# Second attention layer of a four-layer kernel: first rows fetched in the experts' part, split parts stored by feature and stacked in three transfers a side on two queues

## The reference, cut to what matters

```
x = x + attn_a(layernorm(x), ...)      # landmark attention
x = x + ffn(layernorm(x), ...)         # router and three experts
x = x + attn_b(layernorm(x), Wq, Wk, Wv, Wo)
x = x + ffn(layernorm(x), ...)

def attn_b(x, Wq, Wk, Wv, Wo):         # 16 heads of 16 features
    q, k, v = (x @ W.T).reshape(B, T, 16, 16) for W in (Wq, Wk, Wv)
    q, k = apply_rotary(q), apply_rotary(k)
    scores = einsum('bhqd,bhkd->bhqk', q, k) * 16 ** -0.5    # causal mask
    out = einsum('bhqk,bhkd->bhqd', softmax(scores), v)
    return out.reshape(B, T, 256) @ Wo.T
```

## Time and profile before

| | us |
|---|---|
| median of 3 runs (2417.48 to 2418.22) | 2417.69 |
| profiled execution, its time | 2412.47 |
| profiled execution, its span | 2410.7 |
| end of the first experts' stage, start of `layer_b` | 1427.6 |
| first scores of `layer_b` (PE) | 1470.2 |
| first turned scores of `layer_b` (PE) | 1514.4 |
| end of `layer_b` | 1968.0 |

### The profile page before, as it was taken

The page is one execution under the profiler, slowest core; times in us unless marked ns, Lnnn a source line. Parts: engine busy times, 40 slices in busy tenths (PEclk is TensorE's granted clock), DMA queues, the critical chain, the costliest instruction groups (busy, mean ns, idle before and its releaser), DMA issues. The chain is left out here.

```text
span 2410.7 us, 49639 instructions
## 1 busy us (share of the span) xinstructions
PE 2150.9 (89%) x19430; PEld 1743.2 (72%) x19430; DVE 1486.6 (62%) x3884; ACT 1027.4 (43%) x1986; POOL 680.2 (28%) x772
## 2 busy tenths in 40 slices
PE   7799999999999998798789964889999878987998
PEld 7688888888888887677589952445544447766998
DVE  2565664746566474588646645777777628874665
ACT  4343434434343443344245521455555543433554
POOL 3210110201011111266512224433333215662222
PEclk8899999999999999899889987899999989998999
DMA  7300000000000000421657765544455226113775
GB/s 238 119 19 11 10 10 10 19 2 19 10 11 10 10 1 25 110 66 58 241 158 228 236 168 94 90 83 86 84 87 87 43 87 204 42 44 117 231 225 139
DMA packets 155905, 212.84 MB, mean 88 GB/s; under 512 B 51656, under 2 KB 140000, under 8 KB 150368
## 3 DMA queue, kind: packets, MB, share of 16 engines
q1 hardware_dynamic: 142140, 191.51, 27.9%
q0 software_dynamic: 12864, 17.38, 4.4%
q10 hardware_dynamic: 672, 0.79, 0.2%
HBM read 141.93 MB, written 67.69 MB: 87 GB/s over the span
## 5 line engine op out<-in xcount | busy, mean ns | idle before, releaser
L2382 DVE CUSTOM_DVE_ANT_0 bank<-bank,b_raw_masks 128x512 f32<-128x512 f32 (+3 forms) x512 | 239.2, 518 | 140.1 <-PE bank L2609 134.7
L2505 ACT ACTIVATE b_probsT<-bank 128x512 f32<-128x512 f32 x320 | 181.0, 603 | 171.3 <-PE bank L2609 140.1
L2114 PE MATMUL bank<-e_hT_hi,k_rwkv 128*128 128x256 f32 x1088 | 213.0, 282 | 2.8 <-DVE e_hT_lo L2017 2.8
L2114 PEld LDWEIGHTS bank<-e_hT_hi,k_rwkv 128*128 128x128 f32 x1088 | 176.1, 190 | 3.6 <-DVE e_hT_lo L2017 3.6
L2609 PE MATMUL bank<-b_k_stacked,b_q_stacked 96*128 96x512 bf16 (+3 forms) x512 | 127.3, 313 | 54.2 <-DMA b_k_stacked<-scratch_b_parts 26.9
L789 POOL TENSOR_TENSOR probs<-probs,rcp 128x512 f32<-128x512 f32 x64 | 66.9, 1045 | 345.3 <-DVE rcp L658 345.3
L2128 PE MATMUL bank<-v_rwkv_hi,e_hidden_hi 128*128 (+1 forms) x544 | 153.7, 282 | 0.0
L2128 PE MATMUL bank<-v_rwkv_hi,e_hidden_lo 128*128 (+1 forms) x544 | 153.6, 282 | 0.0
L2128 PE MATMUL bank<-v_rwkv_lo,e_hidden_hi 128*128 (+1 forms) x544 | 152.0, 279 | 0.0
L2114 PE MATMUL bank<-e_hT_lo,k_rwkv 128*128 128x256 f32 x544 | 151.5, 279 | 0.0
L2075 ACT ACTIVATE e_relu<-bank,k_bias 128x256 f32<-128x256 f32 x272 | 113.5, 470 | 71.6 <-PE bank L2114 58.0
(11 more groups left out here) (360 smaller groups left out, 6102.7 us busy)
## 6 DMA issues: line engine op xcount, KB each, us to landing
k_rwkv<-scratch_k SPq DMA_DIRECT2D x32, 2048.0 KB, 7.4
scratch_b_parts<-b_part SPq DMA_DIRECT2D x96, 128.0 KB, 1.9
b_q_stacked<-scratch_b_parts SPq DMA_DIRECT2D x96, 128.0 KB, 4.3
b_k_stacked<-scratch_b_parts SPq DMA_DIRECT2D x96, 128.0 KB, 4.4
e_rows<-scratch_rows SPq DMA_DIRECT2D x34, 258.0 KB, 7.6
scratch_rows<-f_hq SPq DMA_DIRECT2D x16, 516.0 KB, 8.4
x_tokens<-in_x_dram SPq DMA_DIRECT2D x8, 512.0 KB, 8.4
scratch_x_out<-x_tokens SPq DMA_DIRECT2D x8, 512.0 KB, 2.9
```

Of the source, the lines that this page charges most:

```text
L2114: last = nc.tensor.matmul(data[:, half * ROWS:(half + 1) * ROWS], ff.k_part(i % 2, a)[:, k, at:at + P], hT[b][:, i % 2, k], start=n == 0, ...
L2382: last = nc.vector.tensor_tensor_reduce(data[:, at:at + size], data[:, at:at + size], raw_masks[:, T - size:T], -1.0, LARGEST, ALU.add, AL ...
L2505: nc.scalar.activation(probsT[:, ring, u], fl.data("st", pair, u)[:], ACT.Exp, scale=DB ** -0.5).then_inc(fl.released("st", pair, u), 1)
```

## The change

Seven edits:

1. `experts`, run 0: SP waits for the same additions as GpSimd and issues x of batch 0 there, on a semaphore of the core, `x_first`, that `layer_b` waits for.
2. Loads of `layer_b`: masks first, on a semaphore of their own; then wq, wk, cosines and sines (`loaded`); then wv and wo (`late_loaded`). ScalarE waits for the masks, PE for the identity alone, the q/k and v products of batch 0 and the maxima for what they read.
3. Batch 0's second q and k products move from slots -8, -7 to -10, -9, its v products from -7, -6 to -10, -9 (`FIRST`, `inputs_at`), with everything that follows them.
4. `parts_out` is laid out [feature, head, token] instead of [head, feature, token]: a feature's eight heads are 8 KB in a row.
5. `Q_PARTS` and `K_PARTS_B` are reordered so that one transfer takes three, two and one parts (`RUNS`). On the q side these are neighbouring parts; on the k side one part repeated 3, 2 and 1 times by a broadcast dimension in front.
6. The first half's stores and stacked transfers: q's on SP's queue, k's on ScalarE's queue, after the middle part of the first keys. Later halves stay on SP.
7. Counts of semaphores follow.

The core of the diff:

```diff
+            if run == 0:
+                for p in range(2):
+                    sp.wait_ge(*added(p, of_parity(p)))
+                sp.dma_start(cols(core.x, 0, XB).rearrange("p (t c) -> p t c", c=C),
+                             x_out[0:T, :].rearrange("(t p) c -> p t c", p=P)).then_inc(core.x_first, 16)
...
-Q_PARTS, K_PARTS_B = (0, 0, 1, 1, 0, 2), (0, 1, 0, 1, 2, 0)
+Q_PARTS, K_PARTS_B = (0, 1, 2, 0, 1, 0), (0, 0, 0, 1, 1, 2)
+RUNS = ((0, 3), (3, 2), (5, 1))
...
+FIRST = {"qk": (-12, -11, -10, -9), "v": (-10, -9)}
 FRONT = {"stats": -15, "xn": -14, "xT": -13, "qk": (-12, -11, -8, -7), "v": (-7, -6), "max": (-2, 2)}
...
-        parts_out, max_out = scratch("b_parts", (B * 4, 3, P, T)), ...
+        parts_out, max_out = scratch("b_parts", (B * 4, 3, DB, HEADS_H, T)), ...
...
-        x_back = [sem(f"b_x_back{n}") for n in range(B)]
+        x_back = [core.x_first] + [sem(f"b_x_back{n}") for n in range(1, B)]
...
+        def inputs_at(slot, kind):
+            first = [(0, i) for i, at in enumerate(FIRST[kind]) if at == slot]
+            return first + [(n, i) for n, i in steps_at(slot, FRONT[kind]) if n]
...
+        by_head = lambda at, c: parts_out[at, c].rearrange("d h t -> h d t")
+        def stack(eng, side, b, at):
+            for first, n in RUNS:
+                src = parts_out[at, 0:n] if side == 0 else parts_out[at, K_PARTS_B[first]].unsqueeze(0).to_broadcast([n, DB, HEADS_H, T])
+                eng.dma_start(stacked[side][b][first * DB:(first + n) * DB, :, :],
+                              src.rearrange("c d h t -> (c d) h t") if side == 0 else src).then_inc(stack_loaded[b], 16)
...
                     for c in range(3):
-                        sp.dma_start(parts_out[at, c], parts[c][:, at % 2]).then_inc(s["parts_stored"], 16)
+                        sp.dma_start(by_head(at, c), parts[c][:, at % 2]).then_inc(s["parts_stored"], 16)
...
-                    for row, c in enumerate((Q_PARTS, K_PARTS_B)[side]):
-                        sp.dma_start(stacked[side][b][row * DB:(row + 1) * DB, :, :],
-                                     parts_out[at, c].rearrange("(h d) t -> d h t", d=DB)).then_inc(stack_loaded[b], 16)
-
-                load_x(0)
+                    stack(sp, side, b, at)
+
+                sp.dma_start(raw_masks[:], dram["masks"]).then_inc(s["masks_loaded"], 16)
+                for dst, name in ((wq, "WqT"), (wk, "WkT")):
+                    sp.dma_start(dst[:], dram[name].rearrange("(k p) n -> p k n", p=P)).then_inc(s["loaded"], 16)
+                for dst, name in ((cos, "cos"), (sin, "sin")):
+                    sp.dma_start(dst[:], dram[name]).then_inc(s["loaded"], 16)
+                for dst, name in ((wv, "WvT"), (wo, "WoT")):
+                    sp.dma_start(dst[:], dram[name].rearrange("(k p) n -> p k n", p=P)).then_inc(s["late_loaded"], 16)
                 core.clear_last(sp)
...
                 for c in range(3):
-                    sp.dma_start(parts_out[0, c], parts[c][:, 0]).then_inc(s["first_stored"], 16)
-                sp.wait_ge(s["keys_split"], 1)
...
-                sp.wait_ge(s["first_stored"], 96)
+                    sp.dma_start(by_head(0, c), parts[c][:, 0]).then_inc(s["first_stored"], 16)
+                sp.wait_ge(s["first_stored"], 48)
+                stack(sp, 0, 0, 0)
...
-                    ready(full("s", pair, u))
+                    ready(full("s", pair, u), (s["masks_loaded"], 16))
...
                     nc.scalar.activation(parts[1][:, at % 2], rotated[:, at % 2], ACT.Copy).then_inc(s["mid_done"], 1)
+                    if (n, step) == FIRST_KEYS:
+                        act.wait_ge(s["keys_split"], 1)
+                        for c in range(3):
+                            act.dma_start(by_head(1, c), parts[c][:, 1]).then_inc(s["keys_stored"], 16)
+                        act.wait_ge(s["keys_stored"], 48)
+                        stack(act, 1, 0, 1)
...
                     if kind in ("qk", "v"):
+                        if n == 0:
+                            pe.wait_ge(*((s["loaded"], LOADS) if kind == "qk" else (s["late_loaded"], LATE)))
...
-                pe.wait_ge(s["loaded"], LOADS)
-                pe.wait_ge(s["consts_done"], CONSTS)
+                pe.wait_ge(core.ident_loaded, 16)
...
+                                pe.wait_ge(s["consts_done"], CONSTS)
+                                pe.wait_ge(stack_loaded[half % STACK_BUFS], STACK_DMAS * 16 * (half // STACK_BUFS + 1))
```

## The result

The changed kernel takes **2565.69 us** (median of 4 runs, 2562.2 to 2567.11) against 2417.95 for the kernel before beside it (4 runs, 2417.48 to 2422.31): 1.0607 times as long, 95% interval 1.0591 to 1.0624. Forecast were 2459 us and a range of 2394 to 2500. The sign was right, and so was the main mechanism, few DMA engines for the k stack; the size was wrong by a factor of 3.6: +148 instead of +41 us.

What follows compares the result with a forecast made beforehand. TensorE was taken to set the steady pace of the second attention layer, with stacked transfers a hidden second bound. Stops of 62 less 15 back gave +47, head -6: +41 us, 2459 us on the median, range 2394 to 2500.

Steps and rivals of the forecast that it cites:

- few DMA engines for the k stack: Stacked k transfers, whose source leads with the repeat, run on 3, 2 and 16 engines: 14.4 us against 7.6.
- a second bound, hidden by 1.7 us of cover: Steady part: first scores of each half need all stacked transfers; a k stack later than 1.7 us stops TensorE, fifteen times.
- The first transfer's packets, 0.45 us each: First k transfer of a stack: 16 packets of 8 KB at 0.45 us, between 0.32 and 0.68, together 7.2 us.
- The rival with full collisions: First k transfer at 0.68 us a packet, SP's later stores caught behind engines 0 and 1: 2515 us, chance 0.05.
- The stores, "1 gained": Steady part: k stores sit less long behind the quicker q stack, 1 us a half gained (0 to 1.4).
- Forecast were 62: Steady part: TensorE's stops over fifteen halves, 15 x 13.4 - 138.8 = 62 us.
- Part comes back: 15: Steady part: VectorE catches up during stops, shortening TensorE's waits for it by about 1 us a half, 15 us.
- The head, -6: Layer's head: first scores stay at 1470.0, but from there to pair 4 takes 20 us instead of 25.75: -6 us.
- the step for the moved work: Head: batch 0's second half and v fill the time before first scores; pair 4 follows after 20 instead of 25.75 us.
- The rival with 16 engines: All stacked transfers use 16 engines, the repeat being folded or split on issue: 2399 us, chance 0.17.

Runs made afterwards that it cites:

- head alone: The changed kernel with the old layout and the old six stacked transfers a side, head edits kept: 2409.15 us, 0.9947 of the kernel before.
- k in pairs: The changed kernel with k's repeated source in runs of 2, 1, 2, 1, so no two engines write 32 partitions apart: 2533.23 us, ratio 1.0459 to before.
- filled waits: The changed kernel with 90 or 45 extra small products before each later half's first scores, their result overwritten: 2539.22 us, 1.0484 of the kernel before.
- parts stored as ready: Old layout and transfers with the head edits, each part stored once rounded instead of after all three: 2403.35 us (0.9922 of before); repeated, 2400.81 us (0.9929).
- ready and filled head: Old transfers with head edits and early part stores, plus 40 small products ahead of the first scores: 2407.65 us, 0.9942 of the kernel before.

## Why the prediction was wrong

Right were: the steady part loses; a second bound, hidden by 1.7 us of cover, sits in the stacked transfers; k's run on 3, 2 and 16 engines; TensorE stops in each of the fifteen halves. That the head gains held only without the new transfers ("head alone"). Wrong were four terms, three of them in the steady part:

- **The first transfer's packets, 0.45 us each.** I took the middle between free and crowded. Two of the three engines collide fully, at about 0.62 once they run evenly: the first transfer takes 9.1 us and not 7.2, and the stack 16.7 and not 14.4. "k in pairs" takes this away, and with one packet more and a crowded start still gains 32.5 us. The rival with full collisions had the mechanism, with a chance of 0.05, and at 2515 us it too fell 50 short, for it kept the next two terms; the Trainium skill's port rule ("SBUF — State Buffer", section "Door 1: The DMA port swizzle"), which I quoted beside 0.45, spoke for it, and was the better guide than a middle value.
- **The stores, "1 gained".** They lead with 8 heads on the DRAM side and use 8 engines. I counted the engines of the new loads and not of the new stores, though I had read in the earlier trace rows that a store of 24 rows uses 12. From the k stores to the k stack are 5.5 us, not 3.1: 2.4 us a half. Together with the stack the landing is 16.7 - 7.6 + 1.4 = 10.5 us later, of which 1.7 were covered: 8.8 x 15 = 132 us of stops were to be expected; the gaps grew by 124.8. Forecast were 62.
- **"Part comes back: 15".** Wrong in sign. The wait for VectorE fell only from 14.3 to 12.8 us, and the stops cost TensorE its clock: 39 us more busy time in the layer for the same work. Of that some 20 us are in the total: beside 124.8 of stops and 7.5 of head there remain 15 us by the medians and 22 by the profiled spans (154.4 less 132.3), and "filled waits" gets 26.5 back. I had read the granted clock as "full" in the earlier trace rows and not asked what would hold it there.
- **The head, -6.** First TensorE work at 1434.64 instead of 1433.0. ScalarE's stores went out at 1451.57 (1449.7) and landed after 7.9 us, not 2.7. The five kernels that store these parts by feature need 5.9 to 8.8 us for it, the four with the old layout ("head alone", "parts stored as ready" twice, "ready and filled head") 4.1 to 4.2. So 1.7 to 4.7 us go with the new layout, and even without it the 2.7 were 1.4 too few. Why the new layout costs so much here is not shown; in the kernel after, 34 of the 408 packets of these stores start only after 1457, beside the q stack that SP issued at 1454.20. The k stack left at 1459.46, hardly earlier than before, and took 18.2 us (17.6 forecast). First scores 1477.70 instead of 1470. From there to pair 4 came 26.7 us instead of 20, with a stop of 6.4 in it. "Head alone" takes 21.3 us to pair 4, so the step for the moved work holds, to 1.3 us, where the transfers don't spoil it.

The two issues of ScalarE's queue at this place, for the kernel after (timeline of ACT):

```profile
1451.57 2.45 ACTq L2543 DMA_DIRECT2D scratch_b_parts<-b_part  x3
...
1459.46 1.97 ACTq L2292 DMA_DIRECT2D b_k_stacked<-scratch_b_parts  x3
```

The rival with 16 engines (2399, chance 0.17) was wrong on the fact. As a price it stands nearer: with 16 engines made by another order of the parts the kernel takes 2414, 15 us more than it said, with the stores on 8 engines still in it; with early stores it takes 2401.

What stays open: how the residue of about 20 us divides between the clock and second effects of the stops (the filling products change both), what delays the head's k stores beyond their 8 engines, and why the profile calls six of the stops "issue".

## What to carry to other kernels

Before transfers are merged, count engines for both sides of every transfer, stores too: in all that were counted here the leading counts of the two sides decided how many of the 16 carry it, and a repeat in front made it 3 or 2. When an order of the data without repeats gives the same sum, it costs nothing and was worth some 150 us here. A wait that appears in every step on the engine that sets the pace cost more than its length here, because the clock fell with it; so price such a stop above its duration, and take nothing off for what other engines might catch up unless a row shows it.

## What the runs showed of the hardware

- A DMA engine alone, with no other 32 partitions away, needs 0.311 us for an 8 KB packet; two engines 32 partitions apart need about 0.62 each (0.615 to 0.65), so the pair gains nothing over one; two engines 16 partitions apart need 0.31 each.
- A transfer with a source repeated 3 or 2 times in front ran on 3 or 2 of the 16 engines, a store whose DRAM side leads with 8 heads on 8.
- 768 KB of k in transfers of 32, 32, 16 and 16 partitions land in 6.5 to 6.7 us, in six of 16 partitions in 7.5 to 8.2, whether in pieces of 1 or of 8 KB. With all engines busy the rate is 238 GB/s in the first and 140 and 133 in the others: here the partitions that are written count, not the size of the piece.
- A stop of TensorE of 5.16 us was followed by 5 us at a granted clock of 0.55, then by 1.00 again; over the layer from 1515 us on that is 0.873 instead of 0.980, and small products that nobody reads, in the stops, bring it to 0.964 and the kernel 26.5 us down.
